# A three-layer feature-interaction kernel: split first loads, a finer last W0 piece, a reordered ramp, ScalarE in place of GpSimd for two stores, and an output on four partitions

## The reference

```
z    = einsum('bid,bjd->bdij', base, curr)       # base = inputs, curr = inputs at first
curr = einsum('bdij,ijh->bhd', z, Wk) + bk       # three times, W0, W1, W2
out  = sum over d of concat(curr1, curr2, curr3) @ lin_w + lin_b
```

## Time and profile before

| | before |
|---|---|
| median of 3 runs | 181.06 us (180.8 to 181.45) |
| the profiled execution's own time | 180.75 us |
| its span | 179.0 us |
| TensorE matmul busy | 173.0 us, 97% |
| VectorE busy | 152.7 us, 85% |
| ScalarE busy | 73.2 us, 41% |
| GpSimd busy | 11.5 us, 6% |
| granted TensorE clock | 0.999 of full speed |
| DMA | 37.58 MB, 210 GB/s in the mean |

### The profile page before, as it was taken

The page is one execution under the profiler, slowest core; times in us unless marked ns, Lnnn a source line. Parts: engine busy times, 40 slices in busy tenths (PEclk is TensorE's granted clock), DMA queues, the critical chain, the costliest instruction groups (busy, mean ns, idle before and its releaser), DMA issues.

```text
span 179.0 us, 2505 instructions
## 1 busy us (share of the span) xinstructions
PE 173.0 (97%) x790; PEld 117.6 (66%) x790; DVE 152.7 (85%) x139; ACT 73.2 (41%) x78; POOL 11.5 (6%) x19
## 2 busy tenths in 40 slices
PE   6799899999999999999999999999999999999994
PEld 2363467777777777777777777777777777777760
DVE  0699886499999999999999999999999999993021
ACT  2556620154642464246433644264426542530021
POOL 3333604000000000000000000000000000000000
PEclk9999999999999999999999999999999999999999
DMA  5999844999878677857785779477957740000000
GB/s 185 385 403 403 283 101 135 421 414 410 292 215 285 172 239 222 309 146 231 226 329 138 233 228 327 139 227 227 285 192 223 233 136 0 0 4 0 0 0 0
DMA packets 12198, 37.58 MB, mean 210 GB/s; under 512 B 2497, under 2 KB 3357, under 8 KB 12190
## 3 DMA queue, kind: packets, MB, share of 16 engines
q1 hardware_dynamic: 11258, 36.91, 62.1%
q10 hardware_dynamic: 868, 0.32, 0.8%
q0 software_dynamic: 64, 0.25, 0.5%
HBM read 36.40 MB, written 1.07 MB: 209 GB/s over the span
## 4 chain that ended last, share of the span: by engine, by line
PE 85%; DMA 6%; SPq 4%; POOL 2%; DVE 1%; ACT 1%; issue 1%; DVEq 0%
PE q_ps L465 42%; PE c_ps L465 41%; DMA pair_sb<-w_pairs 6%; SPq L192 1%; POOL wc_low L433 1%; SPq L188 1%; PE q_ps L474 1%; PE c_ps L605 1%; POOL pair_sb L427 1%; PE c_ps L608 0%; SPq L184 0%; DVE w_post L275 0%; DVE acc L338 0%; ACT out_sb L415 0%; ACT wc_high L368 0%
## 5 line engine op out<-in xcount | busy, mean ns | idle before, releaser
L349 ACT ACTIVATE z_high<-xb_z 126x1024 fp32r<-126x1024 f32 x56 | 59.2, 1061 | 78.8 <-DVE xb_z L254 76.3
L254 DVE TENSOR_TENSOR xb_z<-x_a,xb_z 126x1024 f32<-126x1024 f32 x51 | 62.0, 1216 | 9.6 <-DMA xb_z<-xw 9.5
L261 DVE TENSOR_TENSOR z_low<-xb_z,z_high 126x1024 fp32r<-126x1024 f32 x56 | 68.8, 1234 | 0.0
L465 PE MATMUL c_ps<-z_high,wc_high 126*101 126x512 f32 x112 | 35.3, 396 | 0.4 <-POOL wc_low L433 0.4
L465 PE MATMUL c_ps<-z_low,wc_high 126*101 126x512 f32 x112 | 35.0, 394 | 0.0
L465 PE MATMUL c_ps<-z_high,wc_low 126*101 126x512 f32 x112 | 35.0, 393 | 0.0
L465 PE MATMUL q_ps<-z_high,wq_high 126*101 126x512 f32 x108 | 33.9, 395 | 0.0
L465 PE MATMUL q_ps<-z_high,wq_low 126*101 126x512 f32 x108 | 33.8, 394 | 0.0
L465 PE MATMUL q_ps<-z_low,wq_high 126*101 126x512 f32 x108 | 33.7, 393 | 0.0
L465 PEld LDWEIGHTS c_ps<-z_high,wc_high 126*101 126x101 f32 x112 | 18.3, 165 | 8.8 <-issue 1.0
L465 PEld LDWEIGHTS c_ps<-z_high,wc_low 126*101 126x101 f32 x112 | 18.5, 165 | 7.5
(11 more groups left out here) (59 smaller groups left out, 55.0 us busy)
## 6 DMA issues: line engine op xcount, KB each, us to landing
xb_z<-xw SPq DMA_DIRECT2D x51, 512.0 KB, 4.4
x_a<-xa SPq DMA_DIRECT2D x8, 512.0 KB, 5.0
w_post<-w1x SPq DMA_DIRECT2D x4, 512.0 KB, 8.5
w_d<-w2h SPq DMA_DIRECT2D x4, 404.0 KB, 6.2
pair_sb<-w_pairs SPq DMA_DIRECT2D x1, 404.0 KB, 11.5
d_dram<-w_d SPq DMA_DIRECT2D x2, 189.4 KB, 3.4
d_dram<-w_d SPq DMA_DIRECT2D x4, 94.7 KB, 2.9
pair_sb<-d_dram ACTq DMA_DIRECT2D x3, 82.9 KB
```

The costliest lines, as they stand in the source:

```text
L254: nc.vector.tensor_tensor(xb_z[0:K, c, :], x_a[0:K, u % 2, :], x_b, ALU.mult).then_inc(z_done, 1)
L261: nc.vector.tensor_tensor(z_low[0:K, m % SLOTS, :], xb_z[0:K, c, :], z_high[0:K, m % SLOTS, :].bitcast(fp32), ALU.subtract).then_inc(low_d ...
L349: nc.scalar.activation(z_high[0:K, m % SLOTS, :], xb_z[0:K, m % C, :], ACT.Copy).then_inc(high_done, 1)
L465: last = nc.tensor.matmul(ps[0:J, h * B:(h + 1) * B], w[0:K, c * J:(c + 1) * J], z[0:K, slot, h * B:(h + 1) * B], start=(c == 0 and k == 0 ...
```

## The change

The first x_a is loaded in two halves by SP and the first xb in two halves by ScalarE's queue; VectorE and ScalarE handle chunk 0 and the split of x half by half. `small` is loaded ahead of W0 piece 0. The last W0 piece is cut in two (chunks 3 to 4, and 5 to 6), and GpSimd does sum, sum, low, low on them. The two stores that duplicate parts of D behind group 1 are issued by ScalarE behind its copy of that group, and all ten stores count on one semaphore. TensorE's warm-up is a loop of 14 matmuls, without the fp32 one that followed; select 1 and 2 precede v piece 0, select 5 precedes group 2 of D; VectorE forms chunk 5 before it copies group 2. At the end, the sums over partitions go to four partitions of 128 columns each, by eight matmuls with one-hot columns of ones, and the output copy and store have four rows.

```diff
-DS_SP, DS_POOL = 8, 2
-WC_CUTS = (0, 1, 3, C)
+DS = 10
+WC_CUTS = (0, 1, 3, 5, C)
-WARM = 12
+WARM = 14
+OR = 4
+ON = B // OR
...
-        ones = sb("ones", [J, 1])
+        ones = sb("ones", [J, 2 * OR - 1])
-        out_sb = sb("out_sb", [1, B])
+        out_sb = sb("out_sb", [OR, ON])
...
         def _(sp):
+            def load_first_xa(h, loaded):
+                cols = slice(h * B, (h + 1) * B)
+                sp.dma_start(x_a[:, 0, cols], xa[:, cols]).then_inc(loaded, 16)
...
-            load_xa(0, 0)
-            load_xb(0, 0)
+            load_first_xa(0, xa_first)
+            load_first_xa(1, xa_loaded[0])
+            sp.dma_start(small_sb[:, :], small).then_inc(small_loaded, 16)
             load_w0(0)
-            sp.dma_start(small_sb[:, :], small).then_inc(small_loaded, 16)
...
             load_w0(2)
+            load_w0(3)
...
-            sp.wait_ge(d_stored, 16 * DS_SP)
-            sp.wait_ge(d_stored_pool, 16 * DS_POOL)
+            sp.wait_ge(d_stored, 16 * DS)
...
         def _(dve):
+            def form_first(h, xa_half, xb_half):
+                cols = slice(h * B, (h + 1) * B)
+                dve.wait_ge(xa_half, 16)
+                dve.wait_ge(xb_half, 16)
+                return nc.vector.tensor_tensor(xb_z[0:K, 0, cols], x_a[0:K, 0, cols], xb_z[0:K, 0, cols], ALU.mult)
+
+            def split_x(h):
+                cols = slice(h * B, (h + 1) * B)
+                dve.wait_ge(xa_high, h + 1)
+                nc.vector.tensor_tensor(x_split[LOW_AT:K, cols], x_a[LOW_AT:K, 0, cols],
+                                        x_split[LOW_AT:K, cols].bitcast(fp32), ALU.subtract).then_inc(xa_split, 1)
...
-            form(0, 0)
-            split_x()
+            form_first(0, xa_first, xb_first)
+            split_x(0)
+            form_first(1, xa_loaded[0], xb_loaded[0]).then_inc(z_done, 1)
+            split_x(1)
             split(0, 0)
...
             form(0, 4)
+            form(0, 5)
             copy_d(2)
             split(0, 3)
-            form(0, 5)
             form(0, 6)
...
         def _(act):
-            act.wait_ge(xa_loaded[0], 16)
-            nc.scalar.activation(x_split[0:K], x_a[0:K, 0, :], ACT.Copy).then_inc(xa_high, 1)
+            def load_first_xb(h, loaded):
+                cols = slice(h * B, (h + 1) * B)
+                act.dma_start(xb_z[:, 0, cols], xw[0:128, cols]).then_inc(loaded, 16)
+
+            def round_xa(h, loaded):
+                cols = slice(h * B, (h + 1) * B)
+                act.wait_ge(loaded, 16)
+                nc.scalar.activation(x_split[0:K, cols], x_a[0:K, 0, cols], ACT.Copy).then_inc(xa_high, 1)
+
+            load_first_xb(0, xb_first)
+            load_first_xb(1, xb_loaded[0])
+            round_xa(0, xa_first)
+            round_xa(1, xa_loaded[0])
...
             copy_d(1)
+            act.wait_ge(dgroup_copied, 3)
+            store_d(act, 0, LEFT + F, 0, RIGHT, (32, DR))
+            store_d(act, 1, LEFT - 2 * GI, 0, 2 * GI, (0, 32))
             round_high(0, 3)
             copy_d(3)
             cast_w0(2)
+            cast_w0(3)
...
-            nc.scalar.activation(out_sb[:, :], out_ps, ACT.Identity, bias=const_sb[0:1, 0:1]).then_inc(out_ready, 1)
+            nc.scalar.activation(out_sb[:, :], out_ps, ACT.Identity, bias=const_sb[:, 0:1]).then_inc(out_ready, 1)
...
         def _(pool):
-            nc.gpsimd.memset(ones[:, :], 1.0)
+            nc.gpsimd.memset(ones[:, :], 0.0).then_inc(cleared, 1)
+            pool.wait_ge(cleared, 1)
+            nc.gpsimd.memset(ones[:, OR - 1:OR], 1.0)
...
-            pool.wait_ge(dgroup_copied, 3)
-            store_d(pool, 0, LEFT + F, 0, RIGHT, (32, DR), d_stored_pool)
-            store_d(pool, 1, LEFT - 2 * GI, 0, 2 * GI, (0, 32), d_stored_pool)
             sum_w0(2)
+            sum_w0(3)
             low_w0(2)
+            low_w0(3)
             pool.wait_ge(wc_ready, len(WC_CUTS) - 1)
...
             pe.wait_ge(filled, 1)
-            for _ in range(WARM):
+            with pe.Fori(0, WARM):
                 warm()
-            pe.wait_ge(acc_done, 1)
-            nc.tensor.matmul(warm_ps[0:J, :], acc[:, 0:J], acc[:, 0:B], start=True, stop=True)
-            v_piece(0)
             select_xb(1)
             select_xb(2)
+            v_piece(0)
             v_piece(1)
...
+            select_xb(5)
             d_group(2)
-            select_xb(5)
             d_group(3)
...
-            nc.tensor.matmul(out_ps, ones[:, :], acc[:, 0:B], start=True, stop=False)
-            for i in range(2):
-                pe.wait_ge(last_done, i + 2)
-                last = nc.tensor.matmul(out_ps[:, i * B // 2:(i + 1) * B // 2], ones[:, :],
-                                        prod[:, B + i * B // 2:B + (i + 1) * B // 2], start=False, stop=(i == 1))
+            for i in range(OR):
+                nc.tensor.matmul(out_ps, ones[:, OR - 1 - i:2 * OR - 1 - i], acc[:, i * ON:(i + 1) * ON],
+                                 start=(i == 0), stop=False)
+            for i in range(OR):
+                pe.wait_ge(last_done, 2 + i // (OR // 2))
+                last = nc.tensor.matmul(out_ps, ones[:, OR - 1 - i:2 * OR - 1 - i],
+                                        prod[:, B + i * ON:B + (i + 1) * ON], start=False, stop=(i == OR - 1))
```

More of the change, by code:

```diff
@@ L63 @@
 SEL_AT = LB_AT + 1
-SMALL = SEL_AT + SW
+LW_AT = SEL_AT + SW
+SMALL = LW_AT + OR
 def build(nc, xa, xw, w0_pairs, w1x, w2h, small, out):
@@ L92, in build @@
         v_sb = sb("v_sb", [J, DR])
-        const_sb = sb("const_sb", [1, 1])
-        ones = sb("ones", [J, 1])
+        const_sb = sb("const_sb", [OR, 1])
+        ones = sb("ones", [J, 2 * OR - 1])
         warm_sb = sb("warm_sb", [128, B], mybir.dt.bfloat16)
         acc = sb("acc", [J, N])
-        out_sb = sb("out_sb", [1, B])
+        out_sb = sb("out_sb", [OR, ON])
         spread = small_sb[:, E_AT:E_AT + DR]
-        lw3 = small_sb[0:H, Z_AT + VG:Z_AT + VG + 1]
+        lw3 = small_sb[0:H, LW_AT:LW_AT + OR]
         lw2_row = small_sb[0:H, ROW_AT:ROW_AT + J]
@@ L102, in build @@
         b2 = small_sb[0:H, B2_AT:B2_AT + 1]
-        linb = small_sb[0:1, LB_AT:LB_AT + 1]
+        linb = small_sb[0:OR, LB_AT:LB_AT + 1]
         select_sb = small_sb[0:K, SEL_AT:SEL_AT + SW]
@@ L118, in build @@
         vt_ps = q_ps[1][0:J, B:B + DR]
-        const_ps = q_ps[1][0:1, N - 1:N]
+        const_ps = q_ps[1][0:OR, N - 1:N]
         d_ps = [q_ps[1][:, i * B:i * B + GI * J] for i in range(2)]
-        out_ps = c1_ps[0][0:1, 0:B]
+        out_ps = c1_ps[0][0:OR, 0:ON]
         d_dram = nc.dram_tensor("d_dram", [DR, DW * J], fp32, kind="Internal")
         xb_loaded = [sem(f"xb_loaded{c}") for c in range(C)]
+        xa_first, xb_first = sem("xa_first"), sem("xb_first")
         xa_loaded = [sem(f"xa_loaded{i}") for i in range(2)]
@@ L130, in build @@
         small_loaded, selected = sem("small_loaded"), sem("selected")
-        d_stored, d_stored_pool = sem("d_stored"), sem("d_stored_pool")
+        d_stored = sem("d_stored")
         dpair_loaded = [sem(f"dpair_loaded{i}") for i in range(len(WQ_CUTS) - 1)]
@@ L142, in build @@
         last_sums, last_highs, last_ready = sem("last_sums"), sem("last_highs"), sem("last_ready")
-        filled, equals_cleared = sem("filled"), sem("equals_cleared")
+        cleared, filled, equals_cleared = sem("cleared"), sem("filled"), sem("equals_cleared")
         z_done, high_done, low_done = sem("z_done"), sem("high_done"), sem("low_done")
@@ L163, in gather_d, with store_d @@
                          ).then_inc(dpair_loaded[piece], 16)
-        def store_d(eng, upper, column, first, n, rows, stored=d_stored):
+        def store_d(eng, upper, column, first, n, rows):
             r0, r1 = rows
             eng.dma_start(d_dram[r0:r1, column * J:(column + n) * J],
-                         w2_d[DR * upper + r0:DR * upper + r1, first * J:(first + n) * J]).then_inc(stored, 16)
+                         w2_d[DR * upper + r0:DR * upper + r1, first * J:(first + n) * J]).then_inc(d_stored, 16)
         def chunks(tile, c0, c1):
@@ L238, in _ @@
             sp.wait_ge(out_ready, 1)
-            sp.dma_start(out, out_sb[:, :]).then_inc(out_stored, 16)
+            sp.dma_start(out.rearrange("o (p n) -> (o p) n", p=OR), out_sb[:, :]).then_inc(out_stored, 16)
             sp.wait_ge(out_stored, 16)
@@ L395, in _ @@
                     act.wait_ge(equals_cleared, 1)
-                    act.wait_ge(d_stored, 16 * DS_SP)
-                    act.wait_ge(d_stored_pool, 16 * DS_POOL)
+                    act.wait_ge(d_stored, 16 * DS)
                     for side, t, piece in GATHER:
@@ L503, in select_xb @@
                     pe.wait_ge(select_rounded, 1)
-                    pe.wait_ge(xa_split, 1)
+                    pe.wait_ge(xa_split, 2)
                 if m > 2:
@@ L664 @@
     small[:H, B2_AT] = b2
-    small[0, LB_AT] = lb[0]
+    small[:OR, LB_AT] = lb[0]
+    small[:H, LW_AT:] = lw[2 * H:]
     for first in (0, 2 * P):
```

(2 more changed lines are left out.)

## The result

| | before | changed |
|---|---|---|
| median of 12 runs each | 180.80 us (180.52 to 181.45) | 180.38 us (180.05 to 181.03) |
| ratio, 95% interval | 1 | 0.9970 (0.9957 to 0.9983) |
| a second set, medians of 23 and 12 runs | 181.00 us | 180.50 us |
| ratio, 95% interval | 1 | 0.9977 (0.9955 to 0.9998) |
| the profiled execution, time and span | 180.75, 179.0 us | 180.91, 179.1 us |

The forecast was 181.8. So the two traces show the mechanisms, but their difference (+0.16) isn't that of the medians (-0.42).

The account below looks back on a forecast made before the run. TensorE's unbroken stream bounds the kernel, through q chunk 0's start and the tail. Later q start +1.15 and tail -0.30 give +0.85 us, hence 181.8 us (likeliest case 44%); range 180.5 to 182.2.

Parts of the forecast that it names:

- the landing of the W0 pieces: Cutting the last W0 piece in two would land its halves at about 18.6 and 19.1, the first 0.5 us earlier.
- this sign: Landings of the third W0 piece before 18.1 would show that the forecast had the DMA stream wrong.
- the lock chain: GpSimd's sums and low parts alternate with VectorE's work, memset 24.6, gather 1.3 us late, q chunk 0 1.15 us later.
- The lock itself: When VectorE reads two SBUF operands, it and GpSimd exclude each other from their shared port pair for a whole instruction.
- The copy of group 2 and SP's stores: VectorE's copy, behind form 5, ends 0.7 us later at 18.5; SP's last stores land at about 23.8, not 23.3.
- the first rival: Stores bound the gather: fewer locks, memset by 23.6, SP's later stores decide; 181.0 us, chance 30%.
- The price of that delay: If SP's later stores bound the gather, it comes 0.35 to 0.45 us later and q 0.2 us later.
- Start: Half transfers on two queues and earlier small bring later landings 0.2 us sooner, the matrix v 0.2 to 0.4 us sooner.
- Tail: At the kernel's end the four-row output copy gains 0.33 us, the ones-matmuls cost 0.03: -0.3 us in all.

Follow-up runs that it names:

- h1: The kernel before, unchanged, profiled a second time; that execution took 181.65 us.
- e1: The kernel before with only the two duplicate stores moved from GpSimd to ScalarE, behind its copy of group 1: 181.25 us, ratio 1.0010.
- f1: The kernel before with the new tail, and group 3's two stores issued by ScalarE instead of SP: 180.75 us, ratio 0.9986.
- f2: The changed kernel with group 3's two stores issued by ScalarE instead of SP: 180.59 us, ratio 0.9976.
- j4: The changed kernel with its start undone and the warm-up written out as before: 181.02 us, ratio 1.0008.
- e2: The kernel before with the new tail alone, first time: 180.69 us, ratio 0.9982 to the kernel before.
- Experiment 6: The changed kernel with the third and fourth W0 pieces loaded behind the xb of chunk 6, so they land later: 180.91 us, ratio 0.9999.
- e4: The changed kernel with select 5 again behind group 2 of D, and form 5 behind the copy of group 2 and split 3: 180.60 us, ratio 0.9972.
- g1: The changed kernel with the third and fourth W0 pieces loaded behind the xb of chunk 6: 180.91 us, ratio 0.9999.
- e6: The kernel before with the new tail and the changed order of select 5, form 5 and group 2: 180.67 us, ratio 0.9980.
- experiment 3: The new order of select 5 and form 5 undone in the changed kernel (180.60 us), and added alone to the kernel before with the new tail (180.67 us).
- j1: The kernel before with the new tail and the start's edits, including the warm loop: 180.49 us, ratio 0.9972.
- g2: The changed kernel with its start undone (whole first x from SP, small behind W0 piece 0, selects behind v piece 0), warm loop kept: 181.53 us, ratio 1.0031.
- k1: The kernel before with the new tail alone, second time, run beside the changed kernel: 180.56 us, ratio 0.9972.

## Why the prediction was wrong

- **The failed step is the landing of the W0 pieces**: "half of 404 KB (at 397 GB/s) is 0.5 us earlier, so about 18.6 and 19.1". The first sum began at 17.86 and the second followed without a pause, so both were over by 18.98, ahead of all but the start of split 3. The prediction had named this sign itself ("before 18.1 would mean that I have the DMA stream wrong"). It is the stream in front of the pieces that was mis-sized, not the cut. TensorE's wait for the last w1 piece ended at 18.25 in the trace of before. In the changed kernel the weight load (PEld) waited, and its wait ended here:

```profile
17.28 0.13 PEld L586 LDWEIGHTS q_ps<-w_post,v_sb 101*64 101x64 f32 x1 [0.37 <-DMA w_post<-w1x]
```

  The sum of the whole piece followed 1.01 to 1.04 behind that wait (before, h1, e1, f1), the sum of the first half 0.56 to 0.59 (the changed kernel's three traces, f2, j4): the cut gives the 0.5 of the forecast. The rest is the w1 piece, there at 17.02 to 17.28 in the changed kernel's three traces against 18.25 and 18.61 in the two of before. Why it is sooner stays open: in e2, with the ramp of the kernel before, the whole W0 piece let its sum start at 18.27, while in j4, with the cut, the first half did so only at 18.97. I had taken one execution's landing as exact to 0.3 us, and the lock chain hung on less.
- **Behind it, the chain was also too dear.** Experiment 6 gave it the late landing and measured 0.4 to 0.5 us more than the changed kernel, not 1.15. Left out was that ScalarE holds rounds 4 to 6 behind its cast of the fourth piece: GpSimd's delay stops VectorE too, and the low parts then find the port free. The prediction followed each engine's queue but not this loop back.
- **The lock itself is right**: 1.27 against 2.40 by the neighbours (e4 and the changed kernel), 2.74 for two sums in g1. The rule of the Trainium skill (SBUF — State Buffer, section "SBUF: two separate sides"), that the shared port pair is an exclusive lock for a whole instruction, agrees with the meetings shown here. A rule that holds gave a wrong time, since it needs the meeting, and the meeting needs a landing time.
- **The copy of group 2 and SP's stores**: forecast 18.5 and 23.8, measured 18.71 and 23.56. Two errors cancel in the second number: the last store was issued at 21.37 and not at about 21.1, and landed 2.19 behind that and not 2.7. The mechanism took over, as in the first rival (30%), whose 181.0 on the base of 181.06 would be 180.7 on twelve runs' 180.8; measured 180.4 to 180.5.
- **The price of that delay** (q +0.2) is not to be seen in the medians: order and its undoing change nothing beyond the intervals (e4, e6). That SP's issues are slower when they begin earlier is how the traces lean (experiment 3), not shown for the median run.
- **Start**: forecast 0.2 us sooner, and v 0.2 to 0.4. In the first pair of traces v came at the same time (13.69 on ScalarE against 13.65), and the share of DMA in the first 3 us was 0.30 against 0.36. Over all traces the forecast fares better: the copy of v starts at 13.54 in the mean of the nine with the new start and at 13.95 in that of the eleven with the old one. But less than half of it is left at the gather (23.70 against 23.86), and j1, which has start and tail alone, is not shown to be faster than the tail. Its worth inside the changed kernel (g2) was not foreseen and remains open, as far as it isn't the loop.
- **Tail**: forecast -0.30, measured -0.30 in the traces; for the tail alone the medians fell by 0.2 and 0.4 us (e2, k1), the ratios by 0.3 and 0.5. Right, and with no gain shown for the ramp's edits together it is the result.

No version here is shown to beat the changed kernel; the tail alone equals it within the intervals, with a small part of its edits.

## What to carry to other kernels

Price first what doesn't depend on when a transfer lands: such a term (here the tail, from two rows) held to a few hundredths in the traces, while a chain of four meetings fell with one landing. Where a forecast turns on which of two arrivals is last, look at the spread of arrivals between executions before giving one order the larger chance. When a late engine is followed step by step, follow also who waits for it and thereby clears its way.

## What the runs showed of the hardware that I had not expected

- Between executions of the same kernel the landing of a 240 KB transfer issued at 2.16 moved from about 7.1 to 7.8; q chunk 0 came 0.8 later.
- SP's issue of a 95 KB store took from 0.30 to 1.31 us in the changed kernel; the slow one (19.08) is the second behind the copy of group 2, and the next ones took 0.42 and 0.43. What makes it slow is not shown.
- In f2 the DMA engines moved next to nothing from 22.0 to 24.0, and yet a 25 KB store issued at 19.35 was reported only at 24.0:

```profile
19.35 4.65 DMA d_dram<-w_d
```

A store of SP's in j1, issued at 20.18, took 3.77. The cause of both is open.
